# A state space stage whose skip term becomes a second output product: x times silu(z) made by GpSimd ahead of the scan

## The chip, the cores and the metric

The kernel runs on one core of a Trainium2 chip. A core has five engines that run their own instruction streams and meet only at semaphores: TensorE (PE; matmuls, results to PSUM), VectorE (DVE), ScalarE (ACT), GpSimd (POOL) and SyncE (SP, which here only issues DMA transfers). The metric is the device time of one execution in microseconds (us), lower is better.

## The reference

Four layers follow each other on x of shape (16, 64, 32, 32), each with a residual: a state space layer, a 3x3 convolution, an attention and a shifted sampling with a 1x1 product. The change lies in the first. Cut to what matters:

```python
def _mamba_forward(x, ...):                      # x: normalised, (16, 1024, 64)
    xs, z = jnp.split(einsum('bld,ed->ble', x, W_in), 2, axis=-1)
    xs = silu(causal_conv4(xs) + conv_b)
    dt, Bm, Cm = parts of einsum('bld,ed->ble', xs, W_xproj)
    dt = softplus(einsum('blr,dr->bld', dt, W_dt) + b_dt)
    deltaA = exp(dt[..., None] * A)              # two states per channel
    deltaBx = dt[..., None] * Bm[:, :, None, :] * xs[..., None]
    hst = deltaA * hst + deltaBx                 # scan over the 1024 positions
    ys = sum over states of hst * Ct
    y = ys + xs * D_param                        # the skip term
    y = y * silu(z)
    return einsum('bld,od->blo', y, W_out)
# then a layer norm over the 64 channels, and x = x + the result
```

## The kernel before

**Tiling.** Two images stand above each other on 128 partitions, 64 channels each, so 16 images are 8 pairs (`PAIRS`) of 1024 positions (`L`). A pair is worked in two halves of 512 (`HALF`), because a PSUM bank holds 512 floats. A half is counted as n = 2p + h.

**First stage.** GpSimd makes the normalised input of a pair (`normal`, L1285) and then adds a bias to x (`add_bias`, L1290). TensorE projects it to xs (L1480) and z (L1487). ScalarE reads both out: z through silu into `ZS` (L933), xs for the convolution (L931). VectorE adds three taps (`taps`, L476), reading PSUM. ScalarE puts silu of that into `XS` (L937). Behind the taps VectorE has its setup: a cast, and two rounds of small operations that take the mean off the output weights (the last of a round is L521), then three small ones (L527 to L529).

**State space stage.** It works half by half. For half n:

- TensorE: the dt product (`dt`, L1519), then for the half before it the output product (`project_out`, L1537) and the variance product (`variance`, L1543), then four products for B and C of the half after (`states`, L1526).
- ScalarE: square of the half before (L992, the first instruction of a turn), four softplus steps for the half two on, the inverse deviation of the half before as a logarithm and an exponential (L998, L999), two decay exponentials (`grow`, L985), a logarithm (L978) and two sums.
- VectorE: the input product with B (L544), two scans (L552), the output product with C (L559), the skip (L564: tA += D * xs), a softplus step for the half two on (L536), and for the half before the normalisation (L570) and the residual (L575).
- GpSimd: three softplus operations for a half (`soft`, L1321 to L1324), then `output` for another: the add over the two states (L1330) and the product with silu(z) (L1331), which gives y.

Each engine works its list in order; nothing is reordered at run time. So the result of half n goes once around: VectorE's output product and skip, GpSimd's y, TensorE's output product, ScalarE's square, TensorE's variance product, ScalarE's inverse deviation, and VectorE's normalisation, which stands in VectorE's list between two halves.

The lines around the skip and the output product:

```python
v.scalar_tensor_tensor(tA[h][0], half(XS, p, h), col("dpar"), tA[h][0], ALU.mult, ALU.add)
    .then_inc(s["hc_done"], 1)                       # VectorE, skip
g.wait_ge(s["hc_done"], n + 1)                       # GpSimd, output
link(g.tensor_tensor(tY[h], tA[h][0], tA[h][1], ALU.add))
g.tensor_tensor(tY[h], tY[h], half(ZS, p, h), ALU.mult).then_inc(s["y_done"], 1)
t.wait_ge(s["y_done"], n + 1)                        # TensorE, project_out
mm(product(p, h), mat("wout"), tY[h]).then_inc(s["o_mm"], 1)
```

`R` (12 x 1024 floats a partition) and `WS` are used by the attention stage only and are free in this stage. `TMP` is split into temporaries that only the state space stage uses.

Of the kernel before, what the change touches and what calls it, by code (L numbers as in the profile page):

```python
# [31 lines left out]
L = HH * WW  # L32
# [32 lines left out]
class Chain:  # L65
# [5 lines left out]
    def link(self, ins):  # L71
        self.k += 1
        ins.then_inc(self.sem, 1)
        self.eng.wait_ge(self.sem, self.base + self.k)
# [27 lines left out]
def build(nc, x, pack, out):  # L102
    with ExitStack() as ctx:
# [19 lines left out]
        def mat(name, w=P):  # L123
            return W[:, OFF[name]:OFF[name] + w]

        def col(name, n=P):
            return W[0:n, OFF[name]:OFF[name] + 1]
# [13 lines left out]
        def half(t, p, h):  # L141
            if isinstance(p, int):
                return t[:, p, h * HALF:(h + 1) * HALF]
            return t[:, bass.ds(p, 1), h * HALF:(h + 1) * HALF].rearrange("p a n -> p (a n)")
# [41 lines left out]

        XS = RA
        ZS = RB[:, 0:PAIRS * L].rearrange("p (a n) -> p a n", a=PAIRS)
        TMP = RB[:, PAIRS * L:2 * PAIRS * L]
        G = [TMP[:, b * L:(b + 1) * L] for b in range(2)]  # L190
        AC = [TMP[:, (2 + b) * L:(3 + b) * L] for b in range(2)]
# [60 lines left out]
        def product(p, h):  # L252

            return bank(7 if isinstance(p, int) and (p, h) == (PAIRS - 1, 1) else 5)
# [14 lines left out]
        def stacks_in(n):  # L269
# [26 lines left out]
            stat_ready mean_sq group_mm var_ready pow_done root_done coef_ready  # L296
            g_ready xb_done xz_mm tap_done taps_done silux_done siluz_done
            dt_mm b_mm c_mm o_mm v_mm e_done dta_read u_done dt_read nd_done ln_done dt_done dtx_done
            b_read da_done scan_done c_read hc_done y_done y_last sq_done r_done normed0 blk0_done sums_done
            g1_ready ua_done ub_first ub_done shifted_even shifted_odd moved_even moved_odd conv_mm y1_done w1_mm x1_done  # L300
            minus_done gb_ready z_mm z_read zf_done hi_done lo_done stack_in stack_low asm_mm asm_done v_part v_done
            s_mm s_read m_ready
# [1 line left out]
            g3_pool g3_dve g3_act hat_d hat_abs hat_done am_zero am_in am_dve am_act tr_mm tr_act tr_dve s1_mm s1_copied s2_mm s2_copied  # L304
            bk_mm bk_act bk_dve pw_mm res_done stored""".split()
        s = {n: ctx.enter_context(nc.semaphore(n)) for n in names}
        x_in = [ctx.enter_context(nc.semaphore("x_in%d" % p)) for p in range(PAIRS)]

        block = ctx.enter_context(nc.Block())
# [21 lines left out]
        def _(sp):  # L331
# [20 lines left out]
            for par, of in enumerate((OF_A, OF_B)):  # L352
                one = pack[of, OFF["e12"]:OFF["e12"] + P].rearrange("p (e k c) -> p k e c", e=2, k=2)[:, par]
                sp.dma_start(WE[of, :].rearrange("p (e c) -> p e c", e=2), one).then_inc(s["prelu_in"], 16)

            def stacked(q, b):
                need(sp, s["t_mm"], 32 * q - 64)
# [60 lines left out]
        def _(v):  # L418
# [97 lines left out]
            for par in range(2):  # L516
                q = slice(par * C, (par + 1) * C)
                o = slice(OFF["wout"] + par * C, OFF["wout"] + (par + 1) * C)
                link(v.tensor_reduce(MEANO[q], W[q, o], AX.X, ALU.add))
                link(v.tensor_scalar(MEANO[q], MEANO[q], 1.0 / C, None, ALU.mult))  # L520
                i = v.tensor_scalar(W[q, o], W[q, o], MEANO[q], None, ALU.subtract)  # L521
                if par:
                    i.then_inc(s["wout_done"], 1)
                else:
                    link(i)
            v.wait_ge(s["prelu_in"], 6 * 16)
            link(v.tensor_scalar(OMA, A12, -1.0, 1.0, ALU.mult, ALU.add))  # L527
            link(v.tensor_tensor(AB, A12, B12, ALU.mult))
# [29 lines left out]
                v.wait_ge(s["c_mm"], n + 1)  # L558
                v.tensor_tensor(tAB[h], PS[:, 3:5, :], tBB[h], ALU.mult).then_inc(s["c_read"], 1)  # L559

            def skip(p, h):
                n = 2 * p + h
                v.wait_ge(s["c_read"], n + 1)
                v.scalar_tensor_tensor(tA[h][0], half(XS, p, h), col("dpar"), tA[h][0], ALU.mult, ALU.add)\  # L564
                    .then_inc(s["hc_done"], 1)

            def norm(p, h):
                n = 2 * p + h
                v.wait_ge(s["r_done"], n + 1)
# [7 lines left out]

            def output_last():

                v.wait_ge(s["hc_done"], 2 * PAIRS)  # L580
                v.wait_ge(s["o_mm"], 2 * PAIRS - 2)
                link(v.tensor_tensor(tY[1], tA[1][0], tA[1][1], ALU.add))
                v.tensor_tensor(tY[1], tY[1], half(ZS, PAIRS - 1, 1), ALU.mult).then_inc(s["y_last"], 1)

            def turn(p, h, lead=True, lag=True, tail=False):

                inputs(p, h)
                scan(p, h)
                outputs(p, h)
                skip(p, h)  # L590
                if tail:
                    output_last()
                if lead:
                    soft(p + 1, h)
                if lag:
                    norm(*before(p, h))
                    residual0(*before(p, h))
# [320 lines left out]
        def _(a):  # L918
# [55 lines left out]
            def soft_log(p, h):  # L974
                n = 2 * p + h
                a.wait_ge(s["nd_done"], n + 1)
                need(a, s["b_read"], n - 1)
                act(tU[h], bank(0), ACT.Ln).then_inc(s["ln_done"], 1)  # L978

            def grow(p, h):  # L980
                n = 2 * p + h
                a.wait_ge(s["dt_done"], n + 1)
                need(a, s["y_done"], n - 1)
                for j in range(STATE):
                    i = act(tA[h][j], tM[h], ACT.Exp, scale=ANEG[:, j:j + 1])  # L985
                i.then_inc(s["da_done"], 1)
# [49 lines left out]
            soft_parts(0, 1)  # L1036
            soft(0, 1)
            soft_log(0, 1)
            grow(0, 0)
            turn(0, 0, lag=False)  # L1040
            turn(0, 1)
# [231 lines left out]
        def _(g):  # L1273
# [43 lines left out]
            def soft(p, h):  # L1317
                n = 2 * p + h
                g.wait_ge(s["ln_done"], n + 1)
                g.wait_ge(s["dt_read"], n + 1)  # L1320
                link(g.tensor_tensor(tM[h], tM[h], tU[h], ALU.add))  # L1321
                g.tensor_tensor(tM[h], tM[h], tE[h], ALU.subtract).then_inc(s["dt_done"], 1)
                g.wait_ge(s["dt_done"], n + 1)
                g.tensor_tensor(tU[h], tM[h], half(XS, p, h), ALU.mult).then_inc(s["dtx_done"], 1)  # L1324

            def output(p, h):
                n = 2 * p + h
                g.wait_ge(s["hc_done"], n + 1)
                need(g, s["o_mm"], n - 1)
                link(g.tensor_tensor(tY[h], tA[h][0], tA[h][1], ALU.add))  # L1330
                g.tensor_tensor(tY[h], tY[h], half(ZS, p, h), ALU.mult).then_inc(s["y_done"], 1)  # L1331

            g.wait_ge(s["silux_done"], PAIRS)
            g.wait_ge(s["siluz_done"], PAIRS)
            soft(0, 0)
            soft(0, 1)
            output(0, 0)
            soft(1, 0)
            output(0, 1)
# [124 lines left out]
        def _(t):  # L1464
# [64 lines left out]
            def project_out(p, h):  # L1529
                n = 2 * p + h  # L1530
                if isinstance(p, int) and (p, h) == (PAIRS - 1, 1):
                    t.wait_ge(s["y_last"], 1)
                    t.wait_ge(s["dt_read"], 2 * PAIRS)
                else:
                    t.wait_ge(s["y_done"], n + 1)
                    need(t, s["blk0_done"], n)
                mm(product(p, h), mat("wout"), tY[h]).then_inc(s["o_mm"], 1)  # L1537

            def variance(p, h):
                n = 2 * p + h  # L1540
# [20 lines left out]
            t.wait_ge(s["silux_done"], PAIRS)  # L1561
            turn(0, 0, lag=False)
            t.wait_ge(s["wout_done"], 1)
            turn(0, 1)
            with t.Fori(1, PAIRS - 1) as p:
                turn(p, 0)
# [409 lines left out]
```

## Time and profile before

| | |
|---|---|
| runs shown, median | 700.49 us |
| runs shown, lowest and highest | 698.28 us, 1176.29 us |
| profiled execution, span | 697.9 us |
| PE busy | 625.1 us (90%) |
| DVE busy | 535.1 us (77%) |
| ACT busy | 429.5 us (62%) |
| POOL busy | 385.2 us (55%) |

The span is the time from the first to the last instruction of the profiled execution. The state space stage lies between about 65 and 191 us of it; the first stage ahead of it. A share of busy time over the whole span is a mean over four stages with different limits, so the stage has to be read from its own rows. In these, "x2" is the number of merged instructions, the bracket at the end is the engine's idle time ahead of the row and what ended it.

### The profile page before, as it was taken

Reading aid. Unit: us, or ns where it says so; the run is one execution under the profiler, and the core shown is the slowest. Engines: PE = TensorE matmul, PEld = TensorE weight load, DVE = VectorE, ACT = ScalarE, POOL = GpSimd, SP = SyncE. Lnnn points to the kernel's source line nnn. Section 1 sums busy time; section 2 is a strip of 40 time slices with the busy share of each in tenths; the row PEclk is TensorE's granted clock in tenths of the full one; section 3 lists DMA queues with packets and bytes.
Section 4 is the critical chain, followed back from the end, with each engine's and each line's share of the span. In section 5 each row is a group of like instructions: output and inputs, shape, how many; then the busy total and the mean of one; then the engine's idle time right before and its main releaser. Section 6 shows DMA issues by size and latency. Waiting matters only on the chain.

```text
span 697.9 us, 8622 instructions
## 1 busy us (share of the span) xinstructions
PE 625.1 (90%) x2812; PEld 275.6 (39%) x2812; DVE 535.1 (77%) x857; ACT 429.5 (62%) x737; POOL 385.2 (55%) x243
## 2 busy tenths in 40 slices
PE   3795888888789989999989999999999999986996
PEld 1232332233353332234434444343444444335982
DVE  6996899999934465888858787887878888685547
ACT  2478689899644331235555765748476565787772
POOL 2454788887512140216939779595968979430000
PEclk9997999999999997999989999999999999998999
DMA  9000000000015482404003040300304020200006
GB/s 328 7 0 0 1 0 0 0 0 0 1 45 140 112 199 54 106 1 91 0 1 90 1 91 0 71 21 9 83 0 91 0 31 1 30 1 0 1 1 241
DMA packets 28533, 32.36 MB, mean 46 GB/s; under 512 B 16976, under 2 KB 17104, under 8 KB 28368
## 3 DMA queue, kind: packets, MB, share of 16 engines
q1 hardware_dynamic: 27056, 27.33, 15.3%
q10 hardware_dynamic: 1440, 4.55, 2.7%
q8 instruction: 21, 0.34, 0.2%
q14 instruction: 16, 0.13, 0.1%
HBM read 5.83 MB, written 4.19 MB: 14 GB/s over the span
## 4 chain that ended last, share of the span: by engine, by line
PE 58%; DVE 19%; issue 8%; ACT 7%; POOL 4%; DMA 1%; SPq 1%; DVEq 0%; POOLq 0%; ACTq 0%
PE PS L1723 15%; PE PS L1710 10%; PE PS L1688 9%; PE PS L1599 5%; DVE RB L476 3%; PE PS L1608 2%; PE PS L1677 2%; PE PS L1743 2%; DVE RB L552 2%; DVE PS L544 2%; DVE RB L851 2%; DVE RB L559 1%; PE PS L1850 1%; DVE SM L456 1%; DVE SM L692 1%
## 5 line engine op out<-in xcount | busy, mean ns | idle before, releaser
L692 DVE TENSOR_REDUCE SM<-PS 128x1 f32<-128x512 f32 x256 | 165.0, 683 | 65.3 <-PE PS L1688 64.7
L1154 ACT ACTIVATE RB<-PS 128x512 f32<-128x512 f32 x256 | 138.9, 594 | 88.0 <-PE PS L1710 86.9
L1391 POOL TENSOR_TENSOR RB<-RB 128x1024 f32<-128x1024 f32 x60 | 141.1, 2372 | 7.1 <-DVE RB L721 4.8
L1710 PE MATMUL PS<-R 98*128 98x512 f32 x256 | 95.5, 452 | 1.3 <-ACT RB L1154 1.3
L1688 PE MATMUL PS<-R 96*128 96x512 f32 x256 | 88.7, 418 | 6.9 <-DMA R<-R 3.2
L1723 PE MATMUL PS<-RB 128*64 128x512 f32 x320 | 85.4, 616 | 0.0
L1710 PEld LDWEIGHTS PS<-R 98*128 98x128 f32 x256 | 38.8, 189 | 83.4 <-ACT RB L1154 53.9
L1526 PE MATMUL PS<-RA,W 128*128 (+1 forms) x128 | 63.1, 636 | 8.7 <-DVE RB L552 5.3
L1688 PEld LDWEIGHTS PS<-R 96*128 96x128 f32 x256 | 48.7, 193 | 43.1 <-DVE SM L692 18.9
L1391 POOL TENSOR_TENSOR EX<-EX,RB 128x1024 f32<-128x1024 f32 x24 | 56.5, 2373 | 0.8
L1723 PE MATMUL PS<-RB,RA 128*64 128x512 f32 x192 | 52.7, 627 | 0.0
L1381 POOL TENSOR_TENSOR WS<-RA,WS 128x512 fp32r<-128x512 f32 x12 | 18.7, 1562 | 51.6 <-ACT WS L1129 33.2
L1526 PEld LDWEIGHTS PS<-RA,W 128*128 128x128 f32 x128 | 24.5, 201 | 46.0 <-issue 27.5
L1599 PE MATMUL PS<-RB,WC 128*64 128x512 f32 x168 | 41.7, 613 | 0.9 <-DVE RB L640 0.9
L1091 ACT ACTIVATE RB<-X,SM 64x1024 f32<-64x1024 f32 x15 | 18.5, 1242 | 35.8 <-PE PS L1599 24.4
L552 DVE TENSOR_TENSOR_SCAN RB<-RB,PS 128x512 f32<-128x512 f32 x32 | 38.3, 1237 | 0.6
L1160 ACT ACTIVATE R<-PS 2x512 fp32r<-2x512 f32 x32 | 17.2, 582 | 27.7 <-PE PS L1700 27.7
L456 DVE BATCH_NORM_STATS2 SM<-X 128x6 f32<-128x512 f32 x48 | 31.7, 683 | 1.1 <-DMA X<-x 0.8
L476 DVE SCALAR_TENSOR_TENSOR RB<-PS,W,RB 128x1023 f32<-128x1023 f32 (+2 forms) x24 | 30.6, 1280 | 1.5 <-ACT RB L931 0.8
L1321 POOL TENSOR_TENSOR RB<-RB 128x512 f32<-128x512 f32 x16 | 20.3, 1268 | 16.1 <-ACT RB L978 16.0
L1330 POOL TENSOR_TENSOR EX<-RB 128x512 f32<-128x512 f32 x15 | 19.1, 1277 | 17.8 <-DVE RB L564 17.8
L1723 PEld LDWEIGHTS PS<-RB 128*64 128x64 f32 x320 | 16.2, 135 | 30.6 <-issue 26.5
(186 smaller groups left out, 1111.7 us busy)
## 6 DMA issues: line engine op xcount, KB each, us to landing
R<-WS SPq DMA_DIRECT2D x72, 128.0 KB, 2.4
X<-x SPq DMA_DIRECT2D x8, 512.0 KB, 7.4
RB<-RB SPq DMA_DIRECT2D x32, 128.0 KB, 4.0
RB<-RB ACTq DMA_DIRECT2D x14, 280.5 KB, 4.1
out<-X SPq DMA_DIRECT2D x7, 512.0 KB, 2.7
R<-R SPq DMA_DIRECT2D x20, 128.0 KB, 2.4
W<-pack SPq DMA_DIRECT2D x1, 1072.0 KB, 11.6
R<-R ACTq DMA_DIRECT2D x4, 128.0 KB, 3.3
```

What stands on the lines that cost most here:

```text
L456: return v.bn_stats(BST[:, p, h, :], half(X, p, h))
L476: i = v.scalar_tensor_tensor(AC[b][:, j:L], xp[:, 0:L - j], col("cw%d" % (3 - j)), AC[b][:, j:L], ALU.mult, ALU.add)
L552: i = v.tensor_tensor_scan(tB[h][j], tA[h][j], bank(1 + j), first, ALU.mult, ALU.add)
L692: v.tensor_reduce(MX[:, par, tile, h:h + 1], bank(2 + h), AX.X, ALU.max)\
L1154: act(slot[:, h * HALF:(h + 1) * HALF], bank(4 + h), ACT.Exp).then_inc(s["p_ready"], 1)
L1321: link(g.tensor_tensor(tM[h], tM[h], tU[h], ALU.add))
L1391: i = g.tensor_tensor(out, out, PT[j % SLOTS][par], ALU.add)
L1526: i = mm(bank(1 + 2 * o + j), mat("bc%d" % (2 * o + j)), half(XS, p, h))
L1599: i = mm(conv_out(k, h), WC[:, 3 * k + dx, :], u[:, y, dx:dx + WW], start=(k == 0 and dx == 0), stop=(k == 1 and dx == 2))
L1688: mm(bank(2 + h), stack(b, par, 0)[0:96, tile * P:(tile + 1) * P], stack(b, par, 1)[0:96, h * HALF:(h + 1) * HALF]).then_inc(s["s_mm"], 1)
L1710: mm(bank(4 + h), stack(b, par, 1)[0:98, j * P:(j + 1) * P], stack(b, par, 0)[0:98, h * HALF:(h + 1) * HALF]).then_inc(s["t_mm"], 1)
L1723: i = mm(PS[par * C:(par + 1) * C, h, :], V[b][:, j, par * C:(par + 1) * C], PT[j % SLOTS][par][:, h * HALF:(h + 1) * HALF], start=(j == 0 ...
```

## The change

The skip term leaves VectorE's list. Since y times the weights is linear, W_out applied to (ys + D xs) silu(z) is W_out applied to ys silu(z) plus (W_out D) applied to xs silu(z). The second part becomes a second product of TensorE into the same bank.

- GpSimd makes x times silu(z) of each pair (`gated`, one 128x1024 product): seven of them between the bias adds and its first softplus operation, the eighth after the first two softplus blocks.
- The first seven go to four buffers in `TMP` and from there by a copy that SP issues to `XZ`, which lies in `R`; the eighth goes straight to `WS`. Products 5 to 7 wait for the copy out of the buffer that they reuse.
- VectorE scales the output weights by D (`WOD`, in the place of the input weights), one 128x128 operation in its setup.
- TensorE makes two products into the bank for each half: first `WOD` with `XZ`, then the output weights with y. Both stand behind the wait for y. Ahead of the loop it waits for all copies.
- ScalarE waits for all seven copies ahead of its first decay exponentials, since these overwrite the buffers.
- GpSimd's `output` and VectorE's last one wait for the output product (`c_read`) where they waited for the skip (`hc_done`).

```diff
+        XZ = R[:, 0:PAIRS * L].bitcast(F32).rearrange("p (a n) -> p a n", a=PAIRS)
+        XZLAST = WS[:, 0, :].bitcast(F32)
+        WOD = mat("winx")
+
+        def gate(p):
+            return TMP[:, (4 + p % 4) * L:(5 + p % 4) * L] if p < PAIRS - 1 else XZLAST
...
+            for p in range(PAIRS - 1):
+                sp.wait_ge(s["xs_z"], p + 1)
+                sp.dma_start(XZ[:, p, :], gate(p)).then_inc(xz_in[p % 4], 16)
...
+            v.wait_ge(s["wout_done"], 1)
+            v.wait_ge(s["xz_mm"], 2 * PAIRS)
+            v.tensor_scalar(WOD, mat("wout"), col("dpar"), None, ALU.mult).then_inc(s["wod_done"], 1)
             v.wait_ge(s["prelu_in"], 6 * 16)
...
-            def skip(p, h):
-                n = 2 * p + h
-                v.wait_ge(s["c_read"], n + 1)
-                v.scalar_tensor_tensor(tA[h][0], half(XS, p, h), col("dpar"), tA[h][0], ALU.mult, ALU.add)\
-                    .then_inc(s["hc_done"], 1)
-
...
-                v.wait_ge(s["hc_done"], 2 * PAIRS)
+                v.wait_ge(s["c_read"], 2 * PAIRS)
                 v.wait_ge(s["o_mm"], 2 * PAIRS - 2)
...
                 outputs(p, h)
-                skip(p, h)
                 if tail:
...
             soft_log(0, 1)
+            for k in range(4):
+                a.wait_ge(xz_in[k], 16 * len(range(k, PAIRS - 1, 4)))
             grow(0, 0)
...
             def output(p, h):
                 n = 2 * p + h
-                g.wait_ge(s["hc_done"], n + 1)
+                g.wait_ge(s["c_read"], n + 1)
...
+            def gated(p):
+
+                g.wait_ge(s["silux_done"], p + 1)
+                g.wait_ge(s["siluz_done"], p + 1)
+                if 4 <= p < PAIRS - 1:
+                    g.wait_ge(xz_in[p % 4], 16)
+                g.tensor_tensor(gate(p), XS[:, p, :], ZS[:, p, :], ALU.mult).then_inc(s["xs_z"], 1)
+
+            for p in range(PAIRS - 1):
+                gated(p)
             g.wait_ge(s["silux_done"], PAIRS)
             g.wait_ge(s["siluz_done"], PAIRS)
             soft(0, 0)
             soft(0, 1)
+            gated(PAIRS - 1)
             output(0, 0)
...
-                mm(product(p, h), mat("wout"), tY[h]).then_inc(s["o_mm"], 1)
+                last = isinstance(p, int) and p == PAIRS - 1
+                xz = XZLAST[:, h * HALF:(h + 1) * HALF] if last else half(XZ, p, h)
+                mm(product(p, h), WOD, xz, start=True, stop=False)
+                mm(product(p, h), mat("wout"), tY[h], start=False, stop=True).then_inc(s["o_mm"], 1)
...
             t.wait_ge(s["wout_done"], 1)
+            t.wait_ge(s["wod_done"], 1)
+            for k in range(4):
+                t.wait_ge(xz_in[k], 16 * len(range(k, PAIRS - 1, 4)))
+            t.wait_ge(s["xs_z"], PAIRS)
             turn(0, 1)
```

TensorE's list in the second half of the loop's body, before: the dt product, the output product, the variance product and the products for B and C (out<-in, then the semaphores that the instruction waits for).

```order
L1519 MATMUL PS<-RA,WDT 128x512
L1537 MATMUL PS<-EX,W 128x512 [waits blk0_done,y_done]
L1543 MATMUL PS<-RB,W 128x512 [waits r_done,sq_done]
L1526 MATMUL PS<-RA,W 128x512 [waits scan_done]
L1526 MATMUL PS<-RA,W 128x512
```

And the same place in the changed kernel, whose line numbers are others:

```order
L1540 MATMUL PS<-RA,WDT 128x512
L1560 ISA [waits blk0_done,y_done]
L1560 MATMUL PS<-R,W 128x512
L1561 MATMUL PS<-EX,W 128x512
L1567 MATMUL PS<-RB,W 128x512 [waits r_done,sq_done]
L1547 MATMUL PS<-RA,W 128x512 [waits scan_done]
```

The new product from `R` (L1560) stands between the wait for y and the old product; nothing else moved.

GpSimd's list from the last bias adds to the first add of `output`, before:

```order
L1290 TENSOR_SCALAR X<-X,W 128x1024 [waits g_ready] x2
L1321 TENSOR_TENSOR RB<-RB 128x512 [waits ln_done,dt_read,siluz_done,silux_done]
L1322 TENSOR_TENSOR RB<-RB 128x512 [waits pool_step]
L1324 TENSOR_TENSOR RB<-RB,RA 128x512 [waits dt_done]
L1321 TENSOR_TENSOR RB<-RB 128x512 [waits dt_read,ln_done]
L1322 TENSOR_TENSOR RB<-RB 128x512 [waits pool_step]
L1324 TENSOR_TENSOR RB<-RB,RA 128x512 [waits dt_done]
L1330 TENSOR_TENSOR EX<-RB 128x512 [waits hc_done]
```

And in the changed kernel:

```order
L1300 TENSOR_SCALAR X<-X,W 128x1024 [waits g_ready] x2
L1349 TENSOR_TENSOR RB<-RA,RB 128x1024 [waits siluz_done,silux_done] x4
L1349 TENSOR_TENSOR RB<-RA,RB 128x1024 [waits xz_in0,siluz_done,silux_done]
L1349 TENSOR_TENSOR RB<-RA,RB 128x1024 [waits xz_in1,siluz_done,silux_done]
L1349 TENSOR_TENSOR RB<-RA,RB 128x1024 [waits xz_in2,siluz_done,silux_done]
L1331 TENSOR_TENSOR RB<-RB 128x512 [waits ln_done,dt_read,siluz_done,silux_done]
L1332 TENSOR_TENSOR RB<-RB 128x512 [waits pool_step]
L1334 TENSOR_TENSOR RB<-RB,RA 128x512 [waits dt_done]
...
L1349 TENSOR_TENSOR WS<-RA,RB 128x1024 [waits siluz_done,silux_done]
L1340 TENSOR_TENSOR EX<-RB 128x512 [waits c_read]
```

Seven products stand ahead of the first softplus operation and the eighth ahead of the first add of `output`.

## Rows read from the trace of the kernel before

**Rows 1.** Timeline, VectorE, loop: start us, duration us, engine, line, operation [idle].

```profile
116.60 1.23 DVE L559 TENSOR_TENSOR RB<-PS,RB 128x1024 f32<-128x1024 f32 x1
117.97 0.75 DVE L564 SCALAR_TENSOR_TENSOR RB<-RA,W,RB 128x512 f32<-128x512 f32 x1
118.64 0.68 DVE L536 SCALAR_TENSOR_TENSOR RB<-PS,RB 128x512 f32<-128x512 f32 x1
119.40 0.70 DVE L570 TENSOR_TENSOR PS<-PS,EX 128x512 f32<-128x512 f32 x1
120.26 0.75 DVE L575 SCALAR_TENSOR_TENSOR X<-PS,W,X 128x512 f32 x1 [0.16 <-DVE PS L570]
120.93 1.22 DVE L544 TENSOR_TENSOR PS<-PS,RB 128x1024 f32<-128x1024 f32 x1
...
124.67 1.22 DVE L559 TENSOR_TENSOR RB<-PS,RB 128x1024 f32<-128x1024 f32 x1
...
168.34 1.22 DVE L544 TENSOR_TENSOR PS<-PS,RB 128x1024 f32<-128x1024 f32 x1
```

**Rows 2.** Timeline, ScalarE, the same turns.

```profile
115.11 0.60 ACT L992 ACTIVATE RB<-PS 128x512 f32<-128x512 f32 x1 [0.83 <-PE PS L1537]
...
118.74 0.63 ACT L999 ACTIVATE EX<-EX 128x512 f32<-128x512 f32 x1
...
122.88 0.60 ACT L992 ACTIVATE RB<-PS 128x512 f32<-128x512 f32 x1 [0.58 <-PE PS L1537]
```

**Rows 3.** Timeline, GpSimd, the same turns.

```profile
118.88 1.27 POOL L1330 TENSOR_TENSOR EX<-RB 128x512 f32<-128x512 f32 x1 [1.04 <-DVE RB L564]
120.32 1.27 POOL L1331 TENSOR_TENSOR EX<-EX,RB 128x512 f32<-128x512 f32 x1 [0.16 <-POOL EX L1330]
```

**Rows 4.** Timeline, TensorE, first laps of the stage and the same turns.

```profile
74.77 1.02 PE L1537 MATMUL PS<-EX,W 128*128 128x512 f32 x2
...
81.73 1.06 PE L1537 MATMUL PS<-EX,W 128*128 128x512 f32 x2
...
113.95 1.12 PE L1537 MATMUL PS<-EX,W 128*128 128x512 f32 x2 [0.50 <-POOL EX L1331]
...
116.72 3.70 PE L1526 MATMUL PS<-RA,W 128*128 x8
120.26 1.02 PE L1519 MATMUL PS<-RA,WDT 128*128 x2
121.64 1.12 PE L1537 MATMUL PS<-EX,W 128*128 128x512 f32 x2 [0.36 <-POOL EX L1331]
```

**Rows 5.** Timeline, GpSimd and VectorE, between first stage and state space stage.

```profile
43.77 2.23 POOL L1290 TENSOR_SCALAR X<-X,W 128x1024 f32<-128x1024 f32 x2
...
59.49 0.69 DVE L536 SCALAR_TENSOR_TENSOR RB<-PS,RB 128x512 f32<-128x512 f32 x1 [1.63 <-ACT PS L956]
...
61.05 1.26 POOL L1321 TENSOR_TENSOR RB<-RB 128x512 f32<-128x512 f32 x1 [15.06 <-ACT RB L978]
```

**Rows 6.** Page, costliest groups: line, operation, count | busy us, mean ns.

```profile
L1391 POOL TENSOR_TENSOR RB<-RB 128x1024 f32<-128x1024 f32 x60 | 141.1, 2372 | 7.1 <-DVE RB L721 4.8
```

**Rows 7.** Timeline, VectorE beside GpSimd in the first stage, and VectorE's setup.

```profile
39.05 3.92 DVE L476 SCALAR_TENSOR_TENSOR RB<-PS,W,RB 128x1023 f32<-128x1023 f32 x3 [0.61 <-ACT RB L931]
...
42.59 1.20 POOL L1285 TENSOR_SCALAR RB<-X,SM 128x1024 f32<-128x1024 f32 x1 [1.06 <-PE PS L1487]
...
42.89 0.92 DVE L508 TENSOR_SCALAR SM<-SM 128x2 f32<-128x2 f32 x1
...
56.19 0.25 DVE L521 TENSOR_SCALAR W<-W,SM 64x64 f32<-64x64 f32 x1
...
56.91 0.26 DVE L521 TENSOR_SCALAR W<-W,SM 64x64 f32<-64x64 f32 x1
```

**Rows 8.** DMA issues: out<-in, queue, count, KB each, median us to landing.

```profile
X<-x SPq DMA_DIRECT2D x8, 512.0 KB, 7.4
...
out<-X SPq DMA_DIRECT2D x7, 512.0 KB, 2.7
```

More of the change, by code:

```diff
@@ L298, in build @@
             dt_mm b_mm c_mm o_mm v_mm e_done dta_read u_done dt_read nd_done ln_done dt_done dtx_done
-            b_read da_done scan_done c_read hc_done y_done y_last sq_done r_done normed0 blk0_done sums_done
+            b_read da_done scan_done c_read xs_z wod_done y_done y_last sq_done r_done normed0 blk0_done sums_done
             g1_ready ua_done ub_first ub_done shifted_even shifted_odd moved_even moved_odd conv_mm y1_done w1_mm x1_done
@@ L306, in build @@
         s = {n: ctx.enter_context(nc.semaphore(n)) for n in names}
+        xz_in = [ctx.enter_context(nc.semaphore("xz_in%d" % k)) for k in range(4)]
         x_in = [ctx.enter_context(nc.semaphore("x_in%d" % p)) for p in range(PAIRS)]
```

## The prediction

> **What bounds the kernel now.** I read the views in this order: the timeline of each engine over two turns of the state space loop, to find what each engine waits for; then the same at the head of the stage; then the prices of operations that the change adds.
>
> In the loop VectorE looks like the bound. From the start of one output product to the next its rows follow each other almost without a gap, and the skip term stands among them with 0.75 us [rows 1]. A turn takes 7.90 us: six turns lie between the input products at 120.93 and 168.34. But every other engine waits once in the turn for its neighbour, so there is a ring as well. I follow it from one square on ScalarE to the square two turns on, since the result of half n serves the output of half n+2 by way of VectorE's order. Square at 115.11, the last exponential of the inverse deviation from 118.74 to 119.37 [rows 2]; VectorE's normalisation starts at 119.40, which is 0.03 behind it, so it was waiting for it; then residual, input product, scans, and the output product of the next half at 124.67, which takes 1.22 and ends at 125.89 [rows 1]. From there the rows of the half before give the rest, because the pattern repeats: its output product ended at 117.83, the skip ran from 117.97 to 118.72, and GpSimd's add started at 118.88, that is 1.05 after the output product [rows 1, 3]. From GpSimd's add to TensorE's projection is 2.76 (118.88 to 121.64), from there to the next square 1.24 (to 122.88) [rows 2 to 4]. So the ring comes to 125.89 + 1.05 + 2.76 + 1.24 = 130.94, which is 15.83 after 115.11, or 7.91 per turn. The measured turn is 7.90. **The ring explains the whole turn**; VectorE's own work is only just below it: its normalisation started 0.76 after the operation ahead, which itself had started 0.67 after the skip, so it waited some 0.1.
>
> **The change in the loop.** Removed per half: one operation of 0.75 on VectorE. With the small wait ahead of it the step from output product to the next operation falls from 2.04 (116.60 to 118.64) to about 1.26, so VectorE gains 0.78. On the ring GpSimd's add is now released by the output product itself: of 1.05 there stay the 0.16 that lay between skip and add, so 0.89 leaves the ring.
>
> Added per half: a second 128x128x512 product on TensorE. A product of this kind shows as two matmul rows; eight such rows took 3.54 from 116.72 to 120.26, 0.44 each, so one more product costs 0.88 [rows 4]. Could it lie beside other work? It stands behind the same wait for y as the old product, and the engine works in order, so it can't start while GpSimd still makes y: the whole 0.88 lies between y and the square. **0.89 leaves the ring and 0.88 enters it.** VectorE's gain of 0.78 turns into a longer wait ahead of the normalisation. I take 0 for the loop.
>
> TensorE's own lap has to be looked at too. At the start of the stage it ran one lap with no wait for others, from the projection at 74.77 to the one at 81.73: 6.96. In the loop the lap from projection to the end of the next one's dt product is 120.26 + 0.88 - 113.95 = 7.19, with restarts in it. With 0.88 added these become 7.84 and 8.07 [rows 4], against 7.90. I take 7.84 to 7.90, since a lap that waits for nobody is the first kind, and keep 8.07 as a rival.
>
> **The change at the head.** GpSimd ends its last bias add at 46.00 and was idle until 61.05 [rows 5]. Now it makes seven products of 128x1024. The same operation takes 2.37 [rows 6], so they end at 46.00 + 7 x 2.37 = 62.6. GpSimd's first softplus step, at 61.05 before, can't start earlier: at least +1.6. The lower end is below that only if a 128x1024 product were faster here than in 60 rows elsewhere, which I exclude.
>
> The cover of those 15 us is not free, though. While GpSimd worked from 42.59 to 43.79, a VectorE scalar operation on two columns took 0.92 and ended at 43.81, with GpSimd's; a scalar operation of 64 columns with GpSimd idle took 0.25. The taps, which read PSUM, ran their three operations in 3.92 while GpSimd worked beside them, 1.31 each, and were not held [rows 7]. VectorE's setup starts its first scalar operation of that size at 56.19 and the second at 56.91 [rows 7]. Now they fall into GpSimd's fifth to seventh product (55.5 to 57.85, to 60.2, to 62.6). If each is held to the end of one, the first runs at 57.85, the second (0.72 on) at 60.2, and the new scaling of the output weights, which waits for the second, at 62.6. Then come four small operations including that one, 0.96 by the same 0.72 for three, and VectorE's first softplus step starts at 63.6 where it was at 59.49 [rows 5]: **+4.1**. Unheld, the new operation hides in the time in which VectorE waited for ScalarE there, and +1.6 stands. So the bounds are 1.6 and 4.1. I take 4.1, because the one scalar operation that started under a long GpSimd operation was held to its end.
>
> The Trainium skill, page "SBUF — State Buffer", section "Who interferes with whom", says that a VectorE instruction in a two-port mode or with two SBUF inputs and a GpSimd instruction exclude each other for the whole instruction, whoever starts first. By that rule the sum takes 4.1 and the taps stay free; without it 1.6 would be the term. The trace agrees with it in the 0.92 of the two-column operation.
>
> The seven copies of 512 KB: the same size took 2.7 from SBUF to memory late in the kernel and 7.4 in the crowded load [rows 8]. The last one is issued at 62.6 and lands at 65.3 to 70.0. ScalarE waits for it ahead of its first decay exponentials, behind which stand all its later steps; but in the held case these need GpSimd's two adds first, from 63.6 + 1.56 (59.49 to 61.05) = 65.2 on, so not before 67.7. I take 0 and keep 2.3 for the range. SP's queue has nothing else due before the convolution stage. The eighth product, on GpSimd between two softplus blocks, takes 2.37 where GpSimd was waiting for the first skip; 0 to 1 of it shows.
>
> The first laps of the stage: TensorE's projections at 74.77 and 81.73 carry no wait mark [rows 4], so there no time leaves the ring on GpSimd's side and the product comes in whole: 0.88 for the first, about 0.2 for the second, as VectorE has some slack behind it. At the end of the stage the last half's skip (0.75 and its wait) goes and the last product (0.88) comes: 0.
>
> **Sum.** Profiled span 697.9; head +4.1, first laps +1.1, loop 0, end 0: 703.1. The runs shown have a median of 700.49 and a lowest of 698.28, so 0.4 to 2.6 lie around the span; with 1.4 the time is 704.5.
>
> **The rivals.**
> 1. The head is not held (only +1.6): 702.0. For it: only one held operation is seen, and a short one may start in the gap between two GpSimd operations; against it the 0.92 row. Chance 0.2.
> 2. The skip pays: VectorE sets the turn and the ring has slack. Then 0.78 goes in each of 14 turns, -10.9, and the time is 704.5 - 10.9 - 1.1 = 692.5. For it: VectorE's rows have almost no gaps. Against it: normalisation starts 0.03 behind ScalarE, and GpSimd, TensorE and ScalarE all wait in each turn. It needs the added product to be hidden, which the order of TensorE forbids. Chance 0.12.
> 3. TensorE's lap becomes the bound, with its restarts: 8.07 against 7.90 is 0.17 in 13 turns, +2.2, so 706.7; if GpSimd can't use the earlier release at all (its softplus work for the next half ends too late), the 0.88 comes in whole, 13 x 0.88 = +11.4, 716. This decides for slower from 14 us on, which is 0.7 us more per turn beside the head's 5.2. Against the large form: GpSimd waited for the skip, with its softplus block done at the add at 118.88 (the row's wait mark is 1.04) [rows 3]; the release moves by 0.89, inside that wait. Chance 0.16, most of it near 707 to 710.
> 4. The forecast, 704.5: chance 0.52, own range 701.5 to 707.5.
>
> **How the numbers follow.** A measurement of this kernel tells about 2% (14 us) from no change. Faster by that needs more than VectorE's whole gain, 0.01; slower needs the large form of rival 3, 0.04; the rest, 0.95, is within 2%. The range 697 to 710 holds the forecast, rival 1, the small form of rival 3 and part of rival 2 with an idle head.
>
> **What the changed profile would show.** Right: turn of 7.8 to 8.0; VectorE idle about 0.7 ahead of normalisation, ended by ScalarE's exponential; GpSimd's add about 0.15 behind the output product; projection to square about 2.1; seven GpSimd products of 2.37 from 46 on and setup operations on VectorE of 1 to 2 us each under them; first VectorE softplus step near 63.6. Wrong: a turn near 7.2 (rival 2), a lap on TensorE without a wait near 8.1 (rival 3), setup operations at their old 0.25 (rival 1), or ScalarE idle for a copy.

## The result and the profile after

| | before | after |
|---|---|---|
| median of the runs | 700.06 us | 705.34 us |
| lowest and highest | 698.28 us, 1176.29 us | 704.03 us, 706.22 us |
| profiled execution, span | 697.9 us | 702.2 us |

The ratio is 1.0103, with a 95% interval of 1.0065 to 1.0142: about 1% slower, and near the forecast of 704.5. Slow runs, here the one of 1176.29, are left out of the ratio, which is not that of the two medians above (1.0075) either. The page's lines on the engines, after the change (busy time, share of the span, instructions):

```profile
span 702.2 us, 8700 instructions
PE 632.6 (90%) x2844; PEld 280.5 (40%) x2844; DVE 530.1 (75%) x842; ACT 429.0 (61%) x737; POOL 404.0 (58%) x251
```

VectorE has 5 us less to do, TensorE 7.5 and GpSimd 19 more. These shares don't say where the time went; the state space stage does. I measure it from the start of GpSimd's last bias adds [rows 5] to VectorE's first instruction of the convolution stage, so that a load that came earlier or later doesn't count: **159.20 before, 168.23 after, +9.03**. It has three parts. The way to the first input product (the head) rose from 21.27 to 24.94, +3.67. The two turns behind it rose from 7.42 and 9.06 to 7.55 and 11.19, +2.26. The turn in the loop (a mean over ten) rose from 7.90 to 8.16, +0.26; of the 13 turns left, twelve rose and the last fell by 0.14, 3.03 in all. From the last input product to the end of the stage it is +0.07. So **half of the loss is neither the head nor the extra 0.88 of the forecast's first laps, and the loop, which was to cost nothing, costs most of that**.

The head first. Timeline, VectorE and then GpSimd (columns as in [rows 1]):

```profile
56.21 2.14 DVE L527 CAST IB<-W 128x128 bf16<-128x128 f32 x1
58.39 0.21 DVE L531 TENSOR_REDUCE SM<-W 64x1 f32<-64x64 f32 x1
...
58.82 1.80 DVE L533 TENSOR_SCALAR W<-W,SM 64x64 f32<-64x64 f32 x1
...
61.09 1.84 DVE L533 TENSOR_SCALAR W<-W,SM 64x64 f32<-64x64 f32 x1
62.97 0.29 DVE L540 TENSOR_SCALAR W<-W 128x128 f32<-128x128 f32 x1
...
63.87 0.69 DVE L551 SCALAR_TENSOR_TENSOR RB<-PS,RB 128x512 f32<-128x512 f32 x1
...
46.65 16.23 POOL L1349 TENSOR_TENSOR RB<-RA,RB 128x1024 f32<-128x1024 f32 x7
65.42 1.27 POOL L1331 TENSOR_TENSOR RB<-RB 128x512 f32<-128x512 f32 x1 [2.54 <-ACT RB L986]
```

GpSimd's seven products run to 62.88. VectorE's three larger setup operations end at 58.35, 60.62 and 62.93, each with the end of one of those products (46.65 + 5, 6 and 7 times 2.32 is 58.25, 60.57, 62.89). The scaling behind them, with GpSimd idle, takes 0.29. GpSimd then waits 2.54 for ScalarE, which had itself waited 4.54 for the softplus step of VectorE at 63.87: GpSimd's seven products were done in time, and it was VectorE that came late.

A turn of the loop, timelines of TensorE, ScalarE, VectorE and GpSimd:

```profile
104.63 1.12 PE L1560 MATMUL PS<-R,W 128*128 x2
105.58 1.02 PE L1561 MATMUL PS<-EX,W 128*128 128x512 f32 x2
...
111.69 1.02 PE L1540 MATMUL PS<-RA,WDT 128*128 x2
112.80 1.12 PE L1560 MATMUL PS<-R,W 128*128 x2
...
106.64 0.60 ACT L1000 ACTIVATE RB<-PS 128x512 f32<-128x512 f32 x1 [0.88 <-PE PS L1561]
...
110.27 0.63 ACT L1007 ACTIVATE EX<-EX 128x512 f32<-128x512 f32 x1
...
108.01 1.22 DVE L574 TENSOR_TENSOR RB<-PS,RB 128x1024 f32<-128x1024 f32 x1
109.67 0.69 DVE L551 SCALAR_TENSOR_TENSOR RB<-PS,RB 128x512 f32<-128x512 f32 x1 [0.44 <-ACT PS L964]
110.94 0.70 DVE L579 TENSOR_TENSOR PS<-PS,EX 128x512 f32<-128x512 f32 x1 [0.57 <-ACT EX L1007]
111.81 0.75 DVE L584 SCALAR_TENSOR_TENSOR X<-PS,W,X 128x512 f32 x1 [0.17 <-DVE PS L579]
...
109.39 1.27 POOL L1340 TENSOR_TENSOR EX<-RB 128x512 f32<-128x512 f32 x1 [0.71 <-DVE RB L574]
```

GpSimd's add starts 0.16 behind the output product, as foreseen. VectorE waits twice for ScalarE, 0.44 and 0.57, where neither operation carries a wait mark in [rows 1]. And TensorE's first product of the next half (112.80) starts 0.24 behind the end of the residual (111.81 + 0.75 = 112.56), with no wait mark. That place is the subject of the next experiments.

### The profile page after: what moved, and what is told of

It is laid out like the page before. It is cut to its first block, busy times and chain, and to the rows that moved or that the text cites. A ratio compares the mean times of both kernels' runs of the same rounds, so it can differ in the third digit from the quotient of the medians.

```text
span 702.2 us, 8700 instructions
## 1 busy us (share of the span) xinstructions
PE 632.6 (90%) x2844; PEld 280.5 (40%) x2844; DVE 530.1 (75%) x842; ACT 429.0 (61%) x737; POOL 404.0 (58%) x251
## 4 chain that ended last, share of the span: by engine, by line
PE 70%; DVE 15%; ACT 7%; issue 4%; POOL 2%; DMA 2%; SPq 1%; ACTq 0%; DVEq 0%; POOLq 0%
PE PS L1751 15%; PE PS L1738 10%; PE PS L1716 9%; PE PS L1547 7%; PE PS L1627 5%; DVE RB L488 3%; PE PS L1560 2%; PE PS L1567 2%; PE PS L1705 2%; PE PS L1636 2%; PE PS L1771 2%; PE PS L1561 2%; PE PS L1540 2%; DVE RB L859 2%; PE PS L1878 1%
## 5 line engine op out<-in xcount | busy, mean ns | idle before, releaser
L1379 POOL TENSOR_SCALAR RB<-X,SM 128x1024 f32<-128x1024 f32 x8 | 11.0, 1380 | 30.8 <-DVE SM L640 18.4
```

## The experiments

My theory after the traces: three causes that add up, the held setup, the product in the first laps, and in the loop a **ring through one output bank**. TensorE can't begin a half's new product before the residual of the half before has read the bank. From product to product that is, in the rows above: two products and the way to the square 2.01, square to the end of the inverse deviation 4.26, 0.04 to the normalisation, 0.87 to the residual, 0.75 for it, 0.24 back to TensorE: 8.17, which is the whole turn (104.63 to 112.80). The rival: TensorE's own lap of eight products, which comes to the same moment, since its dt product ends at 112.71. A matmul row is half a product, so "x8" in a row is four products.

**The head alone, the loop alone.** e_head keeps GpSimd's products and copies, but has the skip on VectorE and one output product. e_loop makes no x times silu(z); its second product reads x in its place, so its skip term lacks silu(z).

```diff
# e_head
+                skip(p, h)
...
-                mm(product(p, h), WOD, xz, start=True, stop=False)
...
# e_loop
-            for p in range(PAIRS - 1):
-                gated(p)
...
-                xz = XZLAST[...] if last else half(XZ, p, h)
+                xz = half(XS, p, h)
```

> The head of the change alone: GpSimd makes the eight products and SP copies them, VectorE makes the scaled weights, but the skip stays on VectorE and nobody reads the products. By the hold theory VectorE's setup is stretched and its first softplus step comes 4 to 4.5 us later than in the kernel before, the loop's turn stays 7.90, and the stage ends 4 to 5 us later. If that is carried to the end the time is 704 to 705; if the later stages give back some 4 us whatever the lateness (the changed kernel's stage ended 9.7 late and the span only 4.3), it is about 700.

> The loop of the change alone: skip gone from VectorE, second product on TensorE in each half, but it reads silu(x) itself, so GpSimd makes no products and nothing is copied (the output lacks the gate in the skip term). Both theories of the loop (TensorE's lap, release of the PSUM bank) expect the turn of the changed kernel, 8.16, and a head as before to within 0.5 us; the stage ends about 5 us late. The ring of the forecast alone would have given 7.90. Time 704 to 705 if carried to the end, about 701 if given back.

e_head: 701.99 us, ratio to the kernel before 1.0079 (1.0035 to 1.0123); head 24.96, first turns 7.52 and 9.07, turn 7.90, stage +3.8 where 4 to 5 was expected. e_loop: 701.92, ratio 1.0065 (1.003 to 1.01); head 21.28, first turns 7.60 and 11.19, turn 8.16, stage +5.4. The parts add up, 3.8 + 5.4 = 9.2 against 9.0, and each sits where the theory has it. In e_loop GpSimd is idle under VectorE's setup, and the operations have their short durations again:

```profile
56.76 0.22 DVE L524 CAST IB<-W 128x128 bf16<-128x128 f32 x1
...
57.44 0.25 DVE L530 TENSOR_SCALAR W<-W,SM 64x64 f32<-64x64 f32 x1
```

**No second product at all.** e_noprod leaves out the skip term.

```diff
-                mm(product(p, h), WOD, xz, start=True, stop=False)
-                mm(product(p, h), mat("wout"), tY[h], start=False, stop=True).then_inc(s["o_mm"], 1)
+                mm(product(p, h), mat("wout"), tY[h]).then_inc(s["o_mm"], 1)
```

> The changed kernel without the second product, so the output has no skip term: what VectorE's relief is worth alone. The two-turn ring without skip and without product is 15.83 - 0.89 = 14.94, 7.47 a turn; TensorE's lap and the bank's release lie at 7.0 to 7.3; VectorE's own work at 7.1. Expected 7.5 us a turn, against 8.16, and 9 to 10 us less than the changed kernel: about 696. If VectorE's work had nothing to do with it, the turn stays at 7.9.

696.32, ratio 0.9993 (0.9964 to 1.0022); head 24.95, turn 7.545. So without the skip the turn does fall, by 0.36 and not by VectorE's 0.78: the relief is real, and the 0.88 on TensorE takes all of it and 0.26 more.

**The setup out of GpSimd's way.** e_setup moves the output weights' operations behind VectorE's first turn, the rest behind its second.

```diff
+            out_weights()
...
+            other_setup()
```

> The changed kernel with VectorE's setup moved out from under GpSimd's products: output weights behind the first half of the stage, the rest behind the second. Hold theory: VectorE's first softplus step starts as soon as ScalarE is ready (about 60), GpSimd's right behind its seventh product (about 63 instead of 65.4), the head costs 1.5 to 2 instead of 4.4, time 702.5 to 703. If the head's cost were not the hold, the first softplus step on GpSimd stays at 65.4 and the time at 705.3.

708.6, ratio 1.0173 (1.0135 to 1.0211), where 702.5 to 703 was expected. The head fell to 22.38 (+1.1), but the first two turns rose from 7.55 and 11.19 to 8.77 and 13.28, and the next two by 1.3 together. GpSimd works in those turns as well, and VectorE's timeline shows the operations held again, now on the path to the next input product:

```profile
75.14 1.33 DVE L541 TENSOR_SCALAR W<-W 128x128 f32<-128x128 f32 x1
...
86.78 1.19 DVE L549 TENSOR_TENSOR SM<-SM 128x1 f32<-128x1 f32 x1
88.01 1.38 DVE L550 TENSOR_SCALAR W<-W 128x128 f32<-128x128 f32 x1
```

**Bank or lap.** e_dt puts TensorE's dt product behind the output product, so that its 0.86 no longer stands ahead of the wait for the bank. e_bank frees the bank earlier: the normalisation writes to the bank of the variance, and TensorE waits for it instead of for the residual. e_dtbank does both.

```diff
# e_dt
+                if lag:
+                    project_out(*before(p, h))
                 if lead:
                     dt(p + 1, h)
# e_bank
-                v.tensor_tensor(product(p, h), product(p, h), tR[h], ALU.mult)
+                v.tensor_tensor(bank(6), product(p, h), tR[h], ALU.mult)
...
-                    need(t, s["blk0_done"], n)
+                    need(t, s["normed0"], n)
...
```

> The changed kernel with TensorE's dt product moved behind the output products, where TensorE waits 0.7 us for the square. If TensorE's lap sets the turn (8.16), it falls by 0.6 or more, to the forecast's ring of 7.9. If the release of the PSUM bank sets it (new product, old product, square, inverse deviation, normalisation, residual, and only then the next half's product into the same bank: 0.95 + 1.06 + 4.26 + 0.04 + 0.87 + 0.75 + 0.2 = 8.13 by the rows of the changed kernel), it stays at 8.15.

> The changed kernel with the bank released earlier: the normalisation writes to the bank of the variance, the residual reads it from there, and the next output product waits for the normalisation instead of the residual. Bank theory: 0.75 and more leaves that ring, and the turn falls to the next bound, the forecast's ring of 7.9 or TensorE's lap without waits of 7.85 to 7.95. Lap theory: the turn stays at 8.16.

> Both of these edits. TensorE's lap and the bank's release are then both below 7.5, so what is left is the forecast's two-turn ring with the product in it, 15.82 or 7.9 a turn. If that ring isn't there, the turn falls to 7.5.

e_dt: 713.26 in one run, turn 8.53, neither of the two turns expected. TensorE's own list is free in time now, and the wait for the bank comes into the open:

```profile
122.09 1.12 PE L1560 MATMUL PS<-R,W 128*128 x2 [1.13 <-DVE X L584]
...
125.05 0.69 ACT L952 ACTIVATE RB<-PS,W 128x512 f32<-128x512 f32 x1 [0.34 <-PE PS L1540]
```

It is the residual that releases it. The turn is longer by 0.37 because ScalarE's softplus steps, which stand between square and inverse deviation, now wait for the late dt product (0.34 here, 0.18 in the next turn): that wait is in the same ring. The head was longer too, in this kernel and in e_bank and e_early: 26.4, where the changed kernel had 24.94 and e_noprod, e_dtbank and e_split 24.95 to 24.96 with the same operations in the same order. The cast was held there not to the next end of one of GpSimd's products but past two of them, to the end of the seventh (45.91 to 62.15 in e_dt):

```profile
55.46 6.77 DVE L527 CAST IB<-W 128x128 bf16<-128x128 f32 x1
```

Why it missed two ends in some executions stays open. e_bank: 705.88 in one run, turn 7.97:

```profile
121.72 1.02 PE L1540 MATMUL PS<-RA,WDT 128*128 x2
122.58 1.02 PE L1560 MATMUL PS<-R,W 128*128 x2
...
129.65 1.02 PE L1540 MATMUL PS<-RA,WDT 128*128 x2
130.51 1.02 PE L1560 MATMUL PS<-R,W 128*128 x2
...
128.82 1.29 POOL L1341 TENSOR_TENSOR EX<-EX,RB 128x512 f32<-128x512 f32 x1 [0.16 <-POOL EX L1340]
```

With the bank free, the product follows the dt product at once, and the turn is TensorE's lap, 122.58 to 130.51, 7.93; GpSimd's y was done 0.4 ahead of it (130.11), so the forecast's ring didn't hold it. Both were there, the bank ahead of the lap by 0.2. e_dtbank: 704.25 in one run, turn 8.11 where 7.9 was expected: ScalarE's softplus steps again wait for the late dt product, 0.34 and 0.18 in turn.

**The new product ahead of the wait.** e_early takes e_dtbank and makes the skip's product before it waits for y. e_split leaves dt in its old place instead, and moves one of the two C products of a half into TensorE's wait for the square.

```diff
+                mm(product(p, h), WOD, xz, start=True, stop=False)
                 t.wait_ge(s["y_done"], n + 1)
                 mm(product(p, h), mat("wout"), tY[h], start=False, stop=True)
...
# e_split, behind it
+                    states(p, h, 1, [1])
                 variance(*before(p, h))
```

> Both edits, and the new product stands ahead of the wait for y. Then the 0.88 leaves the two-turn ring: 7.5 a turn, as in the kernel without the second product (7.545). The head still costs 3.7 and the first turns 1 to 2, so the time is 698 to 700, no more than 2 us from the kernel before. If the early product can't be hidden, the turn stays at 7.9 and the time at 703 to 704.

> Bank released by the normalisation, new product ahead of the wait for y, dt product back in its old place, and instead the second C product moved into TensorE's wait for the square. TensorE's lap then has no wait (16 products of 0.43 and restarts, about 7.2), the bank's ring is 7.3, the two-turn ring without the product 7.5: a turn of 7.5 to 7.6, as without the second product. If moving a product into the square's wait delays the ring as the dt product did, the turn stays near 7.9.

e_early: 699.86, ratio 1.0022 (0.9998 to 1.0047), turn 7.73 where 7.5 was expected. e_split: 699.61 in one run, turn 7.537, the 7.545 of the kernel with no second product. **The second product is then free in the loop.** Its lap on TensorE:

```profile
94.65 1.02 PE L1560 MATMUL PS<-R,W 128*128 x2
95.51 1.02 PE L1565 MATMUL PS<-EX,W 128*128 128x512 f32 x2
96.37 1.02 PE L1547 MATMUL PS<-RA,W 128*128 x2
97.23 1.12 PE L1571 MATMUL PS<-RB,W 128*128 128x512 f32 x2
...
101.99 1.02 PE L1560 MATMUL PS<-R,W 128*128 x2
```

The variance product (97.23) has no wait left ahead of it; a C product fills the time that the square takes. e_split has the earlier release of the bank, the early product and the moved C product together; which of them the turn needs was not run apart.

**The setup in VectorE's own waits.** e_setup2 puts the mean of the output weights between the first two softplus steps of VectorE, their scaling behind the second, and the rest behind the second output product. e_best2 is e_split with that setup.

```diff
             soft(0, 0)
+            out_weights()
             soft(0, 1)
+            skip_weights()
...
-            turn(0, 1)
+            turn(0, 1, between=other_setup)
```

> The changed kernel with VectorE's setup in the gaps that its rows show: taking the mean off the output weights between the first two softplus steps, scaling them behind the second, the rest behind the second half's output product, where VectorE waits 3.5 us. Hold theory: the head costs 1.1 (as in the first such attempt) instead of 3.7, and now the first turns stay as in the changed kernel, so the stage ends 2.6 us earlier than there: 702.5 to 703. If the cost only moves, the stage ends as in the changed kernel.

> Both of these together: the second product hidden and VectorE's setup moved. Against the kernel before: head +1.1, first turns +1, 13 turns of -0.35 = -4.6, so the stage ends 2 to 3 us earlier and the time is 0.3 to 0.4% lower than the kernel before. If the head's cost or the clock of the first lap eats it, it is the same to within 0.2%.

e_setup2: 704.75, ratio 1.0102 (1.0064 to 1.0141). The head is 22.38, the first turns 7.54 and 10.6, the stage 2.7 shorter than after the change, as expected; the time is 704.75 against 705.34, not the 702.5 to 703 expected, and does not show it. The stage's own rows tell more here than the time of 700 us around it. e_best2: 696.87, ratio 0.997 (0.9948 to 0.9991), turn 7.536, head 22.36, stage 157.39 against 159.20 before. It beats the kernel before by 0.3%. On VectorE's timeline the operations are still held, but now end before anything needs them:

```profile
62.42 2.97 DVE L534 TENSOR_SCALAR W<-W,SM 64x64 f32<-64x64 f32 x1
...
82.20 1.39 DVE L553 TENSOR_SCALAR W<-W 128x128 f32<-128x128 f32 x1
84.05 0.69 DVE L560 SCALAR_TENSOR_TENSOR RB<-PS,RB 128x512 f32<-128x512 f32 x1 [0.46 <-ACT PS L977]
```

**The clock in the first lap.** Of the 2.26 in the first two turns the product explains 0.86. The rest is in one row of TensorE: after its wait for the first scan its eight rows for B and C (the "eight products" of the expectation below) took 5.32 before and 6.78 after. First row before, then after:

```profile
68.75 5.32 PE L1526 MATMUL PS<-RA,W 128*128 128x512 f32 x8 [4.64 <-DVE RB L552]
```

```profile
73.06 6.78 PE L1547 MATMUL PS<-RA,W 128*128 128x512 f32 x8 [5.47 <-DVE RB L567]
```

The granted clock is the number behind POOL's count in the table by stretch; 0.50 is 1.2 of 2.4 GHz. Before, it fell as the rows began and was back from 72 on; after, it had fallen in the wait and shows 0.50 from 70 to 78. First before, then after:

```profile
68.00:70.00 2.00, 1.25 (x2) 0.73 (x3) 1.93 (x3) 1.92 (x3) 1.08 (x1) 0.66 0.00 0
70.00:72.00 2.00, 2.00 (x3) 0.78 (x3) 1.34 (x2) 0.60 (x1) 1.18 (x1) 0.50 0.03 8
```

```profile
66.00:68.00 2.00, 1.10 (x2) 0.30 (x2) 0.38 (x1) 1.55 (x3) 1.92 (x2) 1.00 0.00 0
68.00:70.00 2.00, 0.00 (x0) 0.00 (x0) 0.91 (x2) 1.66 (x3) 1.92 (x3) 0.76 0.00 0
...
76.00:78.00 2.00, 2.00 (x3) 0.79 (x3) 1.05 (x1) 0.00 (x0) 1.92 (x2) 0.50 0.00 0
...
80.00:82.00 2.00, 2.00 (x6) 0.76 (x4) 1.89 (x2) 0.00 (x0) 1.92 (x2) 1.00 0.00 0
```

e_warm is e_best2 with products in that wait that nothing reads.

```diff
+                for k in range(fill):                # 24 in the first turn
+                    mm(PS[:, 6, 0:P], mat("bc0"), mat("bc0"))
```

> The kernel of e_best2 with 24 products more on TensorE in the first turn, which nothing reads: they go into an unused output bank while TensorE waits for the first scan input, between the dt product and the eight B and C products. Theory (the first lap is longer because TensorE's granted clock fell in its wait): the eight B and C products of the first turn, 6.55 us in e_best2, take 3.6 to 4.5, the granted clock beside them is 0.9 or more, the first turn is 1.5 to 3 us shorter than in e_best2 (10.97 between the second and third input product) and the first convolution instruction behind the stage comes 2 to 3 us sooner after the bias rows (157.4 in e_best2). Rival (the clock is not what makes them long, or it falls whatever TensorE does there): they stay at 6 to 7 and nothing in the turn changes. Time 694 to 696 by the theory, 697 by the rival.

696.0 us, ratio 0.9972 (0.9946 to 0.9997), which the time can't tell from e_best2. TensorE's rows, first e_best2, then e_warm:

```profile
71.78 6.55 PE L1560 MATMUL PS<-RA,W 128*128 128x512 f32 x8 [6.67 <-DVE RB L576]
```

```profile
62.12 5.52 PE L1590 MATMUL PS<-W 128*128 128x128 f32 x48
70.02 5.40 PE L1560 MATMUL PS<-RA,W 128*128 128x512 f32 x8 [2.38 <-DVE RB L576]
```

And the clock of e_warm by stretch:

```profile
68.00:70.00 2.00, 0.00 (x0) 0.00 (x0) 1.97 (x2) 1.97 (x5) 1.92 (x2) 1.00 0.00 0
70.00:72.00 2.00, 1.98 (x4) 1.01 (x5) 1.82 (x2) 1.33 (x3) 2.00 (x2) 0.81 0.00 0
72.00:74.00 2.00, 2.00 (x3) 0.67 (x2) 1.23 (x1) 0.46 (x1) 1.92 (x3) 0.50 0.00 0
74.00:76.00 2.00, 2.00 (x5) 0.91 (x4) 1.97 (x2) 0.00 (x0) 2.00 (x2) 0.84 0.00 0
```

The rows took 5.40 instead of 6.55, and the stage fell by as much (157.39 to 156.29). The first turn is 6.47, where all other kernels but e_setup had 7.15 to 7.62, so the rival, by which nothing changes, falls for that turn. But the turn that I had named, from the second to the third input product, stayed at 10.97, and the expected 3.6 to 4.5 didn't come: the clock stood at 1.00 through the fillers and the 2.38 of wait, and fell only when the rows had begun. Nor does the 5.40 alone show the fillers at work, for without them the same rows took anything from 5.10 to 6.78:

```profile
73.88 5.10 PE L1547 MATMUL PS<-RA,W 128*128 128x512 f32 x8 [5.47 <-DVE RB L567]
```

That is e_noprod, with the same TensorE list up to there and the same wait as after the change. So the low clock makes these rows long, but when it falls and rises I can't say, and that the change itself costs these 1.46 is not shown.

## Why the prediction was right, and where it was not

**The loop: wrong.** "I take 0 for the loop" failed; it costs 0.26 a turn, 3.0 in all. The exchange that it rests on was right: GpSimd's add moved up (0.16 behind the output product, forecast 0.15), projection to square is 2.01 (forecast 2.1), VectorE waits 0.57 ahead of the normalisation (forecast 0.7). By the prediction's own signs the turn (8.16, where 7.8 to 8.0 was right) is outside. What I missed is that this ring was not the only one: of the two waits in TensorE's list ahead of the output product, `y_done` and `blk0_done` (the residual of the half before, see the change's lists), I followed only the first. The ring through the output bank could have been added up from rows that I had: projection to square 1.24, square to inverse deviation 4.26, then 0.03, 0.86, 0.75 [rows 1, 2, 4], and some 0.24 back (the rows of after), 7.38 of a turn of 7.90, so it was in no row's wait. The new product, added to this ring with nothing taken out of it, makes it 8.15 (2.01 in place of 1.24). The residual had been done 0.63 before TensorE's projection began (121.01 and 121.64), less than the 0.88 that the change adds.

**Rival 3** (TensorE's lap, 8.07) came nearest in size, but by the wrong mechanism: with the bank out of the way the lap is 7.93, inside the 7.84 to 8.07 that I gave it. Its sign, a product without a wait mark at a turn near 8.1, came all the same; only e_dt and e_bank told the two apart. Had the bank not been there, the loop would have cost 0.07 a turn. **Rival 2** (VectorE's gain shows) is refuted as the change stands; e_noprod and e_split show that 0.36 of the 0.78 is to be had once the product lies beside other work. My reason against it, that TensorE's order forbids that, holds for the order of this change only: ahead of its wait for y the product needs the free bank, but nothing of y.

**The head: right in its mechanism, its size in part by chance.** Forecast +4.1 by held operations, measured +3.67; rival 1 (+1.6) is refuted, and e_loop shows the same operations short with GpSimd idle. Three holds were counted and three came, but not the same: the cast, for which I counted nothing, was held first (2.14), and the scaling, which I took as held to the end of the seventh product, came behind it and took 0.29. The seven products took 2.32 each, not 2.37. And in three experiments the same operations cost +5.1 to +5.2, with the cast held for 6.77. The Trainium skill, page "SBUF — State Buffer", section "Who interferes with whom", counts casts and scalar operations among those that may shut GpSimd out or be shut out by it, and reductions among those that never do; the trace agrees, with 2.14 and 1.80 against 0.21. (Of VectorE operations with two inputs in SBUF the page says so only against a GpSimd instruction that reads SBUF, as these products do; the prediction put that more widely.) The copies cost nothing, as I took it: no wait of ScalarE for them shows. The end of the stage is nearly unchanged, as forecast (-0.14 in the last turn, +0.07 behind it).

**The first laps: mis-sized.** Forecast 1.1, measured 2.26: the product itself is the 0.86, and 1.46 lies in rows at the lower granted clock, of which I took no account. Since the same rows took 5.10 in e_noprod, this part may belong to the execution and not to the change.

**The number: right partly by luck.** My terms make +5.2, the stage's rows +9.0: missed are 3.0 in the loop and 1.2 in the first laps, less 0.4 in the head, 3.8 in all. The pair of profiles hides that. From the end of the stage on, the execution of before took 494.9 us and that of after 489.5, the highest and the lowest of all profiles here; the experiments lie between, at 490.4 to 494.7. In the table by stretch the clock of before has a dip behind the stage that is deeper than that of after ten microseconds later (before, then after):

```profile
260.00:270.00 10.00, 10.00 (x33) 2.37 (x33) 5.17 (x8) 0.00 (x0) 0.00 (x0) 0.50 0.22 48
```

```profile
270.00:280.00 10.00, 10.00 (x42) 2.51 (x41) 6.30 (x11) 0.20 (x1) 0.00 (x0) 0.83 0.18 40
```

The moment at which the stage ends doesn't decide that: e_best2 ended it at 203.08 and took 490.4 from there, e_split at 203.46 and took 494.3, before at 202.97 and took 494.9. And before alone ran from 692.8 to 701.5 us in the 18 runs beside the first experiments, with mean granted clocks from 0.982 to 0.970. So such differences come from run to run. In time the change costs some 7 us, by the ratio and by the median of those 18 runs (698.11): the terms were 2 us too low, and the base of 699.3 (697.9 + 1.4) about 1 too high, which brought 704.5 so near 705.34.

## What to carry to other kernels

When work is added to a step that several rings pass, each ring has to be summed, also those that carry no wait mark in the trace, and the release of a buffer (here the last reader of an output bank, back to its next writer) is an edge of a ring like any other. An engine's wait becomes cover only if the added work stands ahead of that wait in its list; behind it, it goes into the ring, however idle the engine looks. And work given to an engine that was idle can lengthen its neighbour's operations: look at what stands beside it, not only at what follows.

## What the runs showed of the hardware

- A VectorE operation that is held under GpSimd ended with a GpSimd operation, within 0.1 in every row given here, whatever its own size: a cast went from 0.22 to 2.14, a 64x64 scalar operation from 0.25 to 1.80, and a product of two 128x1 columns from 0.16 to 1.19 in e_setup. The shorter 0.45 and 0.76 of that scalar operation in e_setup are of the same kind: they ended at 73.87 and 75.10, GpSimd's at 73.82 and 75.05. It need not get in at the first end: 2.97 in e_best2 reached past one, 6.77 in e_dt, e_bank and e_early past two.
- The granted clock of TensorE fell to 0.50 during the waits of 5.47 (after) and 6.67 (e_best2), with 0.66 and 0.50 only as it began to work behind 4.64 (before), and while it was already working behind 2.38 (e_warm). The same eight rows (four products) took 5.10 to 6.78 in the kernels without fillers, where eight in the loop take 3.60 to 3.70 at 1.00.
